# A normalized convolution on one core: the first loads change queues, and all but one wait for a constant

## The reference, cut to what matters

```python
def _gn(v, G=16, eps=1e-5):
    B_, C_, H_, W_ = v.shape
    g = v.reshape(B_, G, C_ // G, H_, W_)
    m = jnp.mean(g, axis=(2, 3, 4), keepdims=True)
    s = jnp.var(g, axis=(2, 3, 4), keepdims=True)
    return ((g - m) / jnp.sqrt(s + eps)).reshape(v.shape)
...
fx = jnp.fft.fft2(px, norm='ortho')
wf = jnp.fft.fft2(pw, norm='ortho')
fout = jnp.einsum('bihw,oihw->bohw', fx, wf)
sp = jnp.fft.ifft2(fout, norm='ortho').real
...
sh = (fft_H - out_h) // 2
out = sp[:, :, sh:sh + out_h, sw:sw + out_w]
return out + bias[None, :, None, None]
...
x = x + _L0_conv_ref(_gn(x), L0_conv_weight, L0_conv_bias, 1, 1)
```

## Time and profile before

| | |
|---|---|
| time, median of 3 runs | 83.39 us (83.38 to 83.54) |
| span of the profiled execution, first to last instruction | 82.0 us |
| what lies around the span, by the two numbers above | 1.4 us |
| busy in the span: TensorE, VectorE, ScalarE, GpSimd | 66.8, 50.2, 47.9, 31.6 us |
| bytes moved by the DMA engines | 33.62 MB, 410 GB/s over the span |
| mean granted TensorE clock | 0.959 |

### The profile page before, as it was taken

The page is one execution under the profiler, slowest core; times in us unless marked ns, Lnnn a source line. Parts: engine busy times, 40 slices in busy tenths (PEclk is TensorE's granted clock), DMA queues, the critical chain, the costliest instruction groups (busy, mean ns, idle before and its releaser), DMA issues.

```text
span 82.0 us, 686 instructions
## 1 busy us (share of the span) xinstructions
PE 66.8 (81%) x222; PEld 41.3 (50%) x222; DVE 50.2 (61%) x43; ACT 47.9 (58%) x53; POOL 31.6 (39%) x43
## 2 busy tenths in 40 slices
PE   0009974999999999999999999999999999993000
PEld 0005433566666666666666656666666666660000
DVE  0009936960899499769949995996899324006000
ACT  3307967981699299569947974994798260000000
POOL 6876000004069900106992930490085029400000
PEclk9999998579999999999999999999999999999965
DMA  2899999999979979979959889989979999999995
GB/s 40 299 415 443 463 415 423 447 407 423 551 304 511 479 320 479 511 336 431 511 256 511 383 383 511 447 352 479 463 336 423 423 431 439 431 423 419 397 430 239
DMA packets 2164, 33.62 MB, mean 410 GB/s; under 512 B 296, under 2 KB 330, under 8 KB 500
## 3 DMA queue, kind: packets, MB, share of 16 engines
q1 hardware_dynamic: 2020, 33.36, 96.3%
q0 software_dynamic: 96, 0.19, 0.6%
q10 hardware_dynamic: 48, 0.06, 0.3%
HBM read 16.84 MB, written 16.78 MB: 410 GB/s over the span
## 4 chain that ended last, share of the span: by engine, by line
PE 74%; DMA 14%; DVE 2%; SPq 1%; issue 0%
PE ps L412 73%; DMA x<-x_dram 14%; DVE x L428 2%; PE ps_m L318 1%; SPq L183 1%; PE ps_w L265 0%
## 5 line engine op out<-in xcount | busy, mean ns | idle before, releaser
L412 PE MATMUL ps<-g,w_sb 128*128 128x363 f32 (+1 forms) x192 | 60.7, 473 | 0.1
L412 PEld LDWEIGHTS ps<-g,w_sb 128*128 128x128 f32 x192 | 36.1, 194 | 20.0 <-ACT origin L292 1.4
L283 DVE TENSOR_REDUCE sums<-x 128x1 f32<-128x4096 f32 x7 | 30.9, 4411 | 0.6 <-DMA x<-x_dram 0.6
L394 POOL TENSOR_SCALAR x<-x,bias_sb 128x1984 f32<-128x1984 f32 (+3 forms) x12 | 23.2, 1945 | 18.9 <-ACT origin L292 14.6
L303 ACT ACTIVATE unused<-x,origin 128x4096 f32<-128x4096 f32 (+1 forms) x9 | 30.0, 3330 | 0.3
L428 DVE SCALAR_TENSOR_TENSOR x<-ps,bias_sb,x 128x1089 f32<-128x1089 f32 (+2 forms) x9 | 10.9, 1220 | 7.7 <-PE ps L412 7.7
L373 ACT ACTIVATE g<-x,rstd 128x1089 f32<-128x1089 f32 (+2 forms) x8 | 9.4, 1190 | 3.4 <-DVE rstd L347 3.4
L283 DVE TENSOR_REDUCE first_sums<-x 128x1 f32<-128x2048 f32 x2 | 4.6, 2286 | 6.2 <-DMA x<-x_dram 6.2
L258 POOL COPY sums<-x 128x1 f32<-128x1 f32 x6 | 1.0, 186 | 18.2 <-DMA x<-x_dram 18.2
L335 DVE TENSOR_SCALAR var<-ps_m,square 128x1 f32<-128x1 f32 x8 | 1.8, 219 | 8.2 <-ACT square L330 8.2
L265 PE MATMUL ps_w<-x,avg 128*128 128x1 f32 x4 | 0.9, 304 | 7.1 <-POOL w_sb L476 6.1
(11 more groups left out here) (21 smaller groups left out, 13.3 us busy)
## 6 DMA issues: line engine op xcount, KB each, us to landing
x<-x_dram SPq DMA_DIRECT2D x2, 4096.0 KB, 34.3
out_dram<-x SPq DMA_DIRECT2D x2, 4096.0 KB
x<-x_dram SPq DMA_DIRECT2D x3, 2048.0 KB, 16.0
out_dram<-x SPq DMA_DIRECT2D x3, 2048.0 KB
x<-x_dram SPq DMA_DIRECT2D x2, 1024.0 KB, 6.2
out_dram<-x SPq DMA_DIRECT2D x1, 1056.0 KB
out_dram<-x SPq DMA_DIRECT2D x1, 800.0 KB
out_dram<-x POOLq DMA_DIRECT2D x1, 189.0 KB, 7.7
```

The source lines that it names most:

```text
L283: lambda e: e.tensor_reduce(to_sum(img, k)[:, 0:1], piece, mybir.AxisListType.X, ALU.add),
L394: put("pool", lambda e: e.tensor_scalar(part, part, 1.0, bias_sb, op0=ALU.mult, op1=ALU.add), *free, mark=mark)
L412: lambda e, k=k, dc=dc, rows=rows, top=top: e.matmul(ps[:, 0:rows, 0 : N - dc], w_sb[:, k * P : (k + 1) * P], g[:, top : top + rows, dc:N] ...
```

## The change

The diff touches only the loads. The weights are now issued by SyncE, and the first half of image 0 by ScalarE. The other half of image 0 and the loads of the other images stay on SyncE but are written after the constants, and the second half of image 0 now needs `avg_ok`: SyncE waits until GpSimd has finished the averaging matrix. What follows on SyncE stands behind that wait.

```diff
-    def load(to, of, by="sp"):
+    def load(to, of, *needs, by="sp"):
         name = f"load{len(put.sems)}"
         put.semaphore(name)
-        return put(by, lambda e: e.dma_start(to, of), adds=name)
-
-    loaded[0] = []
-    for half in range(2):
-        rows = slice(half * H // 2, (half + 1) * H // 2)
-        loaded[0].append((rows.stop, load(xts[0][:, rows, :], x[0, :, 0, rows, :])))
-        if half == 0:
-            weights_in = load(wb_sb, wb, by="act")
-    for img in range(1, 4):
-        loaded[img] = [(H, load(xts[img], x[img // 2, :, img % 2]))]
-    for pair in range(2, NPAIR):
-        loaded[2 * pair] = loaded[2 * pair + 1] = [(H, load(pairs[pair], x[pair]))]
+        return put(by, lambda e: e.dma_start(to, of), *needs, adds=name)
+
+    weights_in = load(wb_sb, wb)
+    loaded[0] = [(H // 2, load(xts[0][:, 0 : H // 2, :], x[0, :, 0, 0 : H // 2, :], by="act"))]
...
     put("act", lambda e: e.activation(warm, eps, AF.Sqrt), eps_ok)
+
+    loaded[0].append((H, load(xts[0][:, H // 2 : H, :], x[0, :, 0, H // 2 : H, :], avg_ok)))
+    for img in range(1, 4):
+        loaded[img] = [(H, load(xts[img], x[img // 2, :, img % 2]))]
+    for pair_of in range(2, NPAIR):
+        loaded[2 * pair_of] = loaded[2 * pair_of + 1] = [(H, load(pairs[pair_of], x[pair_of]))]
```

## The result

| | before | after |
|---|---|---|
| time, median of 9 runs each | 83.38 us (83.16 to 83.54) | 83.77 us (83.59 to 84.05) |
| ratio | | 1.0053, 95% interval 1.0037 to 1.0068 |
| span of the profiled execution | 82.0 us | 82.8 us |
| granted clock of TensorE in it | 0.959 | 0.930 |

A forecast was written before the change was run, and what follows sets the result against it. Taken as limit: 33.62 MB of DMA traffic behind the stream's start. Moved queue +0.05, weights 0 and wait 0 gave 82.05 us of span, 83.4 us as time with 1.4 us around it; range 82.95 to 84.0 us.

The forecast's parts named there:

- The bound: Whole kernel: 33.62 MB through the DMA engines, behind the moment the stream comes up to speed, sets the time.
- The 1.5 us: End of the kernel: 624 thousand bytes of older stores queue, so TensorE could be about 1.5 us later at no cost.
- The moved queue: Stream start: image 0's first half issued by ScalarE instead of SyncE, taken as +0.05 us.
- a late ScalarE queue: Stream start: ScalarE's first packet comes 1.45 to 1.5 us after issue, against SyncE's 1.0; +0.45 us.
- a start half as cold: First three microseconds: half of the 0.75 us loss comes back, -0.37 us, 83.0 us; chance 0.29.
- cold stretch: From about 1.75 to 3.0 us: 215 thousand bytes move instead of 534, a loss of 0.75 us.
- The wait: SyncE issues image 0's second half at 3.57 instead of 1.25 us, behind the averaging matrix; taken as 0.
- issue time: SyncE, image 0's second half: issued at 3.57 us, 0.03 us after the averaging matrix is done at 3.54.
- the absence of a gap: DMA engines: second half's packets can flow at 4.6 to 5.05 us, before the first half ends at 5.07; zero gap.
- C: DMA engines, 1.8 to 5.9 us: stream starts late (+0.45) or resumes cold (+0.47); 83.85 us, 84.3 for both; chance 0.24.
- Rival D: TensorE limits: halves share engines, first half lands at 6.46 instead of 5.99, convolutions 0.15 us later; 83.6 to 83.8; chance 0.07.
- half clock: TensorE after 13.8 us: a further stretch at 1.2 GHz of 2.4 would make the time about 83.8 us.

The follow-up runs named there:

- the late store: First pair's store issued one image later, in the kernel before and in the kernel after: 84.00 us (1.0048) and 84.32 us (1.0040).
- after with the trigger: Kernel after with the last pair loaded in two pieces and the first store held until the first piece has landed: 83.28 us, 0.9993.
- smaller packets: Last two pairs loaded as four images, 16 KB packets instead of 32 KB, in before and in after: 83.87 us (1.0063) and 84.24 us (1.0104).

## Why the prediction was right or wrong

**The number and the account.** The time lies in the range. That is luck in part: the sum came 0.4 us too low, and the account behind it, that neither part of the change costs anything, did not hold.

**The bound** was right in the main: the number of bytes behind the start of the stream, not TensorE, against the chain of waits. The kernel with fewer products shows it. The 1.5 us that TensorE was said to have to spare are too many: in the first trace after its additions end 1.4 us later than before, and the span is 82.8 us against 82.5 in the second.

**The moved queue**, taken at +0.05 us, measured +0.1 with an interval that includes zero (1.0011, 0.9993 to 1.0029). Both of its bounds, a late ScalarE queue (+0.45) and a start half as cold (-0.37), were too far out. (The cold stretch was reckoned from 1.75 us, where no packet moves up to 1.82; from there it loses 0.68 us and not 0.75.) In the trace after, ScalarE's queue shows its first packet between 2.00 and 2.05 us, 1.2 us after the issue. The net is small, but the parts are not by the rows: a lead of 0.2 to 0.3 us up to 39 us, and a dearer switch behind it.

**The wait** was the step that failed: "I take 0". It measured 0.3 to 0.4 us (wait alone 1.0045; after against the queues without the wait, 0.27 us in medians). The issue time, 3.56 us, and the absence of a gap were right; what was wrong is that an absent gap means no cost. Two costs showed in its place. One was named as C's: the late transfer's first packets are slow though the engines are busy. It was priced at 0.47 us and measured 0.13 us at this wait (377 against 434 GB/s), and 0.54 us at a wait 0.47 us longer. C had it begin when the first packets come later than 5.07 us. With the issue at 3.56 they could flow from 4.6 on, by the prediction's 1.0 us, and a part of the cost is there already; the whole of it is there with the issue at 4.03, and so with packets from 5.0 on.

The other was in no rival. The sum took the rate of the stream behind its start as fixed. It is not: between 39 and 70 us the kernels with either part of the change move 417 to 420 GB/s, and the two traces of before 422 and 424. In the change as a whole that is as much as the difference in time. The place is the switch from the last load to the first store. It was in the traces of before too, a row of 1.66 at 40 to 41 us, and the prediction, which averaged from 3 to 81 us, did not look there.

**What is shown, and what only indicated.** Shown: that the wait costs, by the two partial kernels and the longer wait; and that the queued store slows the last load's packets, by the late store, which removes it in both kernels. Indicated: that the change's cost comes mainly out of that switch. For it speak that before and after are level up to 39 us, the equal landings at 42.6 us without the queued store, after with the trigger at 0.9993, and the rates from 39 to 70 us with the store still queued: 419, 417, 418, 420 and (smaller packets) 419 GB/s in the traces with some of the change, 424, 422 and (smaller packets) 426 in those without. Against it speak two kernels. The kernel with fewer products has 419 there, and from 39 to 42 us 350 GB/s at a share of 1.07, a loss of 0.77 us, with the old start and, in its median, the time of before. The kernel with the queues without the wait has 418 and a loss of 0.91, and costs 0.1 us, which can't be told from none. Both are one trace each, and the switch of one kernel moves by 0.24 us between two traces. Why the start of the loads should make the switch at 40 us dearer stays open; an unlike offset of the 16 engines to each other is a rival that was not tried.

**Rival D** did not decide, though its 83.6 to 83.8 us hold the number; that is chance. Its premise, that the engines take from both queues in turn, would have delayed the first half; with both halves in flight in two queues the first landed at 5.83 us, no later. Its half clock did turn up twice as long in the profiled execution and belongs to the longest runs, not to the median.

## What to carry to other kernels

When the DMA engines are busy from end to end, a wait put ahead of the loads has nothing to win by itself, and it costs before it opens a gap. Here a second transfer issued 3.8 us ahead of the end of the first cost nothing at its start, 1.5 us ahead 0.13 us, and 1.0 us ahead 0.54 us (in one long execution). Look at the DMA rate in short stretches where the kind of transfer changes, from loads to stores above all, even when the share is 1 throughout: a share over 1 at a lower rate is packets that take longer. A store that is queued behind a load can slow the load. Issuing it by a landing shortly before the loads' end, rather than as early as its data allow, is worth a trial: it took after from 1.0059 to 0.9993, and before from 1.0001 to 1.0029, so see where the gain is given back.

## What was not expected of the hardware

- Two transfers on SyncE's and ScalarE's queues, issued 0.45 us apart, landed one after the other (5.83 and 8.31 us) and not side by side. The small transfer of the weights did flow beside a large one: from 2 to 3 us SyncE's queue has 29 packets there and ScalarE's 25.
- A queued store took the last 32 KB packets of a load from 1.22 us to 1.66 and 1.98 us on the mean; with 16 KB packets the span was not shorter.
- A transfer issued at 4.03 instead of 3.56 us, behind one that ended at about 5.1, started at 188 instead of 377 GB/s (one long execution).
- Leaving out a quarter of TensorE's products moved the last store's issue from 76.09 to 72.62 us and the time by nothing.
